# Eight 32 by 64 places of the array at once, and 32 by 32 turns, in the setup of an attention kernel

## The chip, the cores and the metric

The kernel runs on one core of a Trainium2 chip. The metric is the time of one execution on the device, in microseconds (us). The core has five engines that run their own instruction streams and meet in semaphores: TensorE (PE, with its weight loads shown apart as PEld), VectorE (DVE), ScalarE (ACT), GpSimd (POOL) and SyncE (SP), whose queue starts most of the DMAs.

## The reference

One transformer layer over x of shape (4, 1024, 128), all in float32: attention with 16 heads of 64 and a bias by distance, a layer norm, a gated feed-forward part with a token shift, and a second layer norm. Each part's result is added to its input ahead of its layer norm.

```python
q, k, v = jnp.einsum('bsx,xMnd->Mbnsd', x, qkv)
a = jnp.einsum('bnsd,bntd->bnst', q, k) * q.shape[-1] ** (-0.5)
cum = jnp.cumsum(rpe_bias[:, :s], axis=-1)
bias = jnp.where(rel >= 0, cum[:, jnp.clip(rel, 0)], PAD)
a = jax.nn.softmax(a + bias, axis=-1)
mix = jnp.einsum('bnst,bntd->bnsd', a, v)
return jnp.einsum('bnsd,ndx->bsx', mix, out_w)
...
x_prev = jnp.concatenate([jnp.zeros((B, 1, C), x.dtype), x[:, :-1, :]], axis=1)
xr = mu_r * x + (1.0 - mu_r) * x_prev
xk = mu_k * x + (1.0 - mu_k) * x_prev
r = jax.nn.sigmoid(jnp.einsum('btc,dc->btd', xr, W_r))
k = jnp.einsum('btc,dc->btd', xk, W_k)
k_act = jnp.square(jax.nn.relu(k))
out = r * jnp.einsum('btc,dc->btd', k_act, W_v)
```

## The kernel before

The work is cut into 32 pair steps: 4 batches by 8 pairs of heads. Each step has 16 slots, one for each head and each tile of 128 query rows. In a slot TensorE makes the scores of a row tile four slots ahead (L1098), VectorE adds the bias and takes the row minimum (L769), ScalarE takes the exponential (L567), TensorE transposes the result (L1115), VectorE and ScalarE empty the banks (L787, L585), and TensorE multiplies with v (L1139) and projects q, k and v of the next pair (L1073, L1078). The order is written out by hand in one function for each engine, and every engine's stream starts with its part of the setup. All 32 steps stand behind that setup: whatever makes it longer or shorter moves them as a block.

The setup is the stretch that the change touches. These are its parts, in the order in which TensorE runs them:

- L1001: two turns of the relative bias (16 rows). L738 on VectorE copies the result.
- L1008: eight transposes of 128 by 128 that turn the tiles of x, four for each half. They wait for the two DMAs of x. L745 on VectorE and L612 on ScalarE copy the halves to `x_cur`.
- L1013: two products with only 16 output rows, the running sum of the bias. L747 copies the result, SP writes it to DRAM (L343) and reads it back in shifted rows as the bias table (L339).
- L1054: the projections of the first pair ("twin"), four of them, then the first scores (L1098), then four more. They need `x_cur` and the weights that L741 on VectorE lays out.

VectorE's stream before the change is: two memsets of the bias row (L734, L735), the copy L738, the two copies of L741, L745, L747, and then the low parts of the first pair (L848, L852) between the first bias rows (L769).

A float32 product stands in the profile as two matmul records and two weight loads; a transpose of float32 data in L1008 is one record.

Of the kernel before, what the change touches and what calls it, by code (L numbers as in the profile page):

```python
# [10 lines left out]
HEADS, D, SPAN = 16, 64, 256  # L11
P = 128
PAIRS = HEADS // 2
PAIR_STEPS = BATCH * PAIRS
TILES = SEQ // P
GROUP = 4
NEAR = SPAN + P
FAR = SEQ - NEAR
BANK = 512
# [5 lines left out]

ROWS = [(h, i) for g in range(TILES // GROUP) for h in range(2) for i in range(GROUP * g, GROUP * g + GROUP)]
NROWS = len(ROWS)
# [13 lines left out]
def score_at(r):  # L41


    if r < NROWS // 2:
        return BANK * (r % 4)
    width = P * (ROWS[r][1] + 1)
    return SEQ * (r % 2) + ((SEQ - width) // 2 if width - BANK < SHORTEST else 0)


def score_end(r):  # L50
    return score_at(r) + P * (ROWS[r][1] + 1 if ROWS[r][1] >= GROUP else GROUP)

# [42 lines left out]
def build(nc, x, qkv, out_w, rpe, w_r, w_k, w_v, mu_r, mu_k, out):  # L95


    seq_d = nc.dram_tensor("bias_by_distance", (HEADS, 4 * P), F32, kind="Internal").ap()
    toeplitz = bass.AP(seq_d.tensor, 0, [[4 * P, HEADS], [1, P], [1, NEAR]])
    mix_d = nc.dram_tensor("mix_transposed", (PAIR_STEPS, P, SEQ), F32, kind="Internal").ap()  # L100
    inv_d = nc.dram_tensor("inverse_sums", (2, 2, 2 * GROUP, P), F32, kind="Internal").ap()
    xt_d = nc.dram_tensor("x_transposed", (BATCH, P, SEQ), F32, kind="Internal").ap()
# [7 lines left out]
    with ExitStack() as ctx:  # L110
        def sb(name, shape, dt=F32):
            return ctx.enter_context(nc.sbuf_tensor(name, shape, dt))

        def ps(name, shape):
            return ctx.enter_context(nc.psum_tensor(name, shape, F32))

        def sem(name):
            return ctx.enter_context(nc.semaphore(name))
# [6 lines left out]
        ident = sb("ident", [P, P])  # L125
# [15 lines left out]
        inv = sb("inv", [P, NROWS])  # L141
        inv_t = [sb(f"inv_t{g}", [2 * GROUP, P]) for g in range(2)]
        inv_all = [sb(f"inv_all{g}", [P, GROUP * P]) for g in range(2)]
        pt = [[sb(f"pt{h}{g}", [P, GROUP * (g + 1), GROUP * P]) for g in range(2)] for h in range(2)]
        mix_sb = [sb(f"mix_sb{g}", [P, GROUP * P]) for g in range(2)]
# [40 lines left out]
        ps_rows = ps("ps_rows", [P, 2 * SEQ])  # L186
# [8 lines left out]
        s_const = sem("const")  # L195
# [18 lines left out]
        s_w_twin = sem("twin_weights")  # L214
        s_twin = sem("twin_projected")
        s_twin_hi = sem("twin_hi_ready")
        s_twin_lo = sem("twin_lo_ready")
        s_stack = [sem(f"stacked{h}") for h in range(2)]
        s_table = [[sem(f"table{a}{h}") for h in range(2)] for a in range(2)]
# [108 lines left out]
        def _(sp):  # L328
# [7 lines left out]
            def load_table(n):  # L336

                for h in range(2):
                    sp.dma_start(table[n % 2][:, h, 0:NEAR], toeplitz[n % PAIRS * 2 + h, :, :])\  # L339
                        .then_inc(s_table[n % 2][h], 16)  # L340
# [133 lines left out]
        def _(pool):  # L474
# [11 lines left out]
            for a in range(2):  # L486
                pool.memset(table[a][:, :, NEAR:], 0.0).then_inc(s_zero, 1)
            pool.memset(x1_t[:, 0:1], 0.0).then_inc(s_zero, 1)
# [233 lines left out]
        def _(dve):  # L722
# [11 lines left out]
            nc.vector.memset(seq_sb[:, 0:P - 1], MASKED).then_inc(s_seq, 1)  # L734
            nc.vector.memset(seq_sb[:, P - 1 + SPAN:], 0.0).then_inc(s_seq, 1)  # L735

            dve.wait_ge(s_rpe_t, 1)
            nc.vector.tensor_copy(rpe_t, ps_t[0][:, 0:2 * HEADS].rearrange("p (a n) -> p a n", a=2)).then_inc(s_rpe_t, 1)  # L738
            dve.wait_ge(s_w[0], 16)
# [256 lines left out]
        def _(pe):  # L996
# [3 lines left out]
            for a in range(2):  # L1000
                ins = nc.tensor.transpose(ps_t[0][:, HEADS * a:HEADS * a + HEADS],  # L1001
                                          pt[0][0][0:HEADS, 0, P * a:P * a + P], ident[0:HEADS, 0:HEADS])
            ins.then_inc(s_rpe_t, 1)

            for first in (0, GROUP):
                pe.wait_ge(s_in_x[first // GROUP], 16)
# [5 lines left out]
            for a in range(2):  # L1012
                ins = nc.tensor.matmul(ps_t[1][0:HEADS, 0:SPAN], rpe_t[:, a, :], above[:, a, :],  # L1013
                                       start=(a == 0), stop=(a == 1))
# [88 lines left out]
            def transpose(n, r, tile_too):  # L1103
                pe.wait_ge(s_exp, NROWS * n + r + 1)
                for k in (k for k in range(NBANKS) if BANKS[k][0] == r):
                    _, b0, nb = BANKS[k]

                    if TBANK[k] == 2 and 2 not in TBANK[:k]:
                        pe.wait_ge(s_raw, 2 * n + 2)
                    else:  # L1110
                        engine, count = emptied(n, k)
                        pe.wait_ge(s_ev[engine], count)
                    for b in range(nb):
                        at = P * (b0 + b)
                        ins = nc.tensor.transpose(t_bank[TBANK[k]][:, P * b:P * b + P].bitcast(F32R),  # L1115
                                                  prob_r[:, r % PSLOTS, at:at + P], ident_r[:, :])
                    if k in INV_BANK:
                        g = INV_BANK.index(k)
                        pe.wait_ge(s_inv, 2 * n + g + 1)
                        ins = nc.tensor.transpose(t_bank[TBANK[k]][0:2 * GROUP, 3 * P:],  # L1120
                                                  inv[:, 2 * GROUP * g:2 * GROUP * (g + 1)], ident[:, :])
                    if k == X1_BANK and tile_too:
                        pe.wait_ge(s_chain, CH * (n - TILE_LAG + 1) + 4)
                        ins = nc.tensor.transpose(t_bank[TBANK[k]][:, P:2 * P], x1[:, :], ident[:, :])
                    ins.then_inc(s_tr, 1)
# [171 lines left out]
```

## Time and profile before

| | before |
|---|---|
| median of the runs | 1114.47 us (1114.06 to 1114.88, 2 runs) |
| the profiled execution | 1114.79 us |
| its span on the core | 1113.0 us |
| TensorE matmul busy | 1062.6 us, 95% of the span |
| TensorE weight loads | 751.8 us, 68% |
| ScalarE | 779.6 us, 70% |
| VectorE | 753.3 us, 68% |
| GpSimd | 97.3 us, 9% |

The span runs from the first instruction to the last; 1.8 us of the execution's time lie around it. Busy time of TensorE counts overlapping matmuls once. "Released by" in a row is what ended the idle time ahead of it. Times in rows are us from the span's start, and a row may hold several instructions of one line, merged: it then gives the start of the first and the time that all of them cover.

### The profile page before, as it was taken

What the parts mean: (1) busy time and instruction counts of PE and PEld (TensorE: products, weight loads), DVE (VectorE), ACT (ScalarE), POOL (GpSimd) and SP (SyncE); (2) the same over time, 40 slices, a digit from 0 to 9 for tenths busy, and PEclk for the clock granted to TensorE, in tenths of its full rate; (3) what the DMA queues carried; (4) which work ended last, traced back from release to release, by engine and by line L of the source; (5) the groups of instructions that cost most, each with busy time, mean ns of one, the idle gap of its engine ahead of it and who ended that gap; (6) DMA issues with size and microseconds to landing.
All of it is one profiled execution on the core that took longest, in us unless ns stands there. A gap on an engine that the chain in (4) does not pass through costs nothing.

```text
span 1113.0 us, 21807 instructions
## 1 busy us (share of the span) xinstructions
PE 1062.6 (95%) x6983; PEld 751.8 (68%) x6983; DVE 753.3 (68%) x1983; ACT 779.6 (70%) x2002; POOL 97.3 (9%) x103
## 2 busy tenths in 40 slices
PE   7899999999999999999999999999999999999995
PEld 4665666666666777676777676677676677666774
DVE  5665556666666777676777776767766667776667
ACT  4766677776767777777777776777676777777743
POOL 1000000000000111000011100011100011100100
PEclk9999999999999999999999999999999999999997
DMA  3765575675667677667676666776766676765810
GB/s 96 182 152 161 162 178 143 167 185 135 163 156 175 163 169 171 167 157 182 162 179 159 173 155 160 170 181 167 178 153 159 166 185 148 184 158 151 245 61 21
DMA packets 114319, 177.58 MB, mean 160 GB/s; under 512 B 13312, under 2 KB 72592, under 8 KB 114208
## 3 DMA queue, kind: packets, MB, share of 16 engines
q1 hardware_dynamic: 111648, 175.08, 63.2%
q10 hardware_dynamic: 2560, 1.12, 0.4%
q8 instruction: 58, 0.95, 0.4%
q14 instruction: 53, 0.43, 0.1%
HBM read 58.41 MB, written 20.22 MB: 71 GB/s over the span
## 4 chain that ended last, share of the span: by engine, by line
PE 61%; DMA 6%; ACT 5%; SPq 5%; issue 4%; DVE 3%; POOL 1%; DVEq 0%
PE ps_o L1139 19%; PE ps_rows L1098 15%; PE ps_t L1115 8%; PE ps_m L1073 7%; DMA stacks<-k_lo 6%; PE ps_m L1155 4%; SPq L323 4%; PE ps_m L1078 3%; ACT prob L567 3%; PE ps_o L1115 2%; ACT pt L585 2%; POOL mix_sb L496 1%; DVE pt L787 1%; PE ps_rows L1200 1%; SPq L388 1%
## 5 line engine op out<-in xcount | busy, mean ns | idle before, releaser
L769 DVE CUSTOM_DVE_ANT_0 prob<-ps_rows,table 128x128 f32<-128x128 f32 (+7 forms) x512 | 379.9, 750 | 96.6 <-PE ps_rows L1098 84.6
L567 ACT ACTIVATE prob<-prob,low 128x128 f32<-128x128 f32 (+7 forms) x512 | 394.4, 772 | 41.1 <-DVE low L769 37.0
L1098 PE MATMUL ps_rows<-stacks 128*128 128x512 f32 (+3 forms) x1536 | 393.4, 367 | 11.3 <-DMA stacks<-k_lo 9.3
L1115 PE MATMUL ps_t<-ident_r,prob_r 128*128 128x128 f32 x1984 | 282.9, 262 | 6.5 <-ACT pt L585 2.5
L1115 PEld LDWEIGHTS ps_t<-ident_r,prob_r 128*128 128x128 f32 x1984 | 212.2, 141 | 87.3 <-issue 71.4
L1139 PE MATMUL ps_o<-pt,v_pair 128*64 128x512 f32 (+3 forms) x1536 | 269.8, 493 | 0.0
L1098 PEld LDWEIGHTS ps_rows<-stacks 128*128 128x128 f32 x1536 | 244.5, 189 | 32.9 <-DMA stacks<-k_lo 13.9
L787 DVE COPY pt<-ps_t 128x512 f32<-128x512 f32 (+3 forms) x288 | 165.1, 583 | 147.1 <-PE ps_t L1115 146.9
L1139 PEld LDWEIGHTS ps_o<-pt,v_pair 128*64 128x64 f32 x1536 | 102.0, 137 | 177.1 <-issue 164.8
L585 ACT ACTIVATE pt<-ps_t 128x512 f32<-128x512 f32 (+3 forms) x384 | 175.1, 456 | 32.3 <-PE ps_t L1115 31.4
L496 POOL TENSOR_TENSOR mix_sb<-mix_sb,inv_all 128x512 f32<-128x512 f32 x64 | 82.2, 1284 | 922.0 <-ACT mix_sb L609 922.0
L1073 PE MATMUL ps_m<-x_cur,w_cur 128*128 128x512 f32 x248 | 129.4, 603 | 5.6 <-ACT x_t L539 2.6
L552 ACT ACTIVATE q_hi<-ps_m 128x512 fp32r<-128x512 f32 x62 | 36.7, 592 | 120.1 <-PE ps_m L1073 119.8
L567 ACT ACTIVATION_READ_ACCUMULATOR prob<-prob,low 128x1 f32 x512 | 98.3, 192 | 0.0
L755 DVE SCALAR_TENSOR_TENSOR q_lo<-ps_m,q_hi 128x512 fp32r<-128x512 f32 x62 | 42.8, 691 | 53.3 <-ACT q_hi L552 53.3
L1078 PEld LDWEIGHTS ps_m<-w_cur,x_cur 128*128 128x128 f32 x504 | 65.5, 191 | 3.2 <-issue 0.5
L1078 PE MATMUL ps_m<-w_cur,x_cur 128*128 128x128 f32 x504 | 66.3, 274 | 0.0
L583 ACT ACTIVATE inv_t<-ps_t 8x128 f32<-8x128 f32 x64 | 16.8, 262 | 63.2 <-PE ps_o L1139 59.5
L1073 PEld LDWEIGHTS ps_m<-x_cur,w_cur 128*128 128x128 f32 x248 | 42.2, 188 | 17.0 <-issue 7.2
L1115 PE MATMUL ps_o<-ident_r,prob_r 128*128 128x128 f32 x320 | 43.9, 252 | 5.4 <-DVE pt L787 5.3
L755 DVE SCALAR_TENSOR_TENSOR k_lo<-ps_m,k_hi 128x512 fp32r<-128x512 f32 x62 | 42.7, 689 | 7.1 <-ACT k_hi L552 4.7
L1155 PE MATMUL ps_m<-wo,mix_tile 128*128 128x128 f32 x384 | 47.0, 275 | 0.0
(131 smaller groups left out, 690.8 us busy)
## 6 DMA issues: line engine op xcount, KB each, us to landing
stacks<-k_hi SPq DMA_DIRECT2D x124, 256.0 KB, 4.5
stacks<-k_lo SPq DMA_DIRECT2D x124, 256.0 KB, 5.0
inv_all<-inverse_sums SPq DMA_DIRECT2D x128, 128.0 KB, 3.2
stacks<-q_hi SPq DMA_DIRECT2D x62, 256.0 KB, 3.7
stacks<-q_lo SPq DMA_DIRECT2D x62, 256.0 KB, 4.3
mix_transposed<-mix_sb SPq DMA_DIRECT2D x62, 256.0 KB, 3.7
table<-bias_by_distance SPq DMA_DIRECT2D x64, 192.0 KB, 3.8
mix_tile<-mix_transposed SPq DMA_DIRECT2D x24, 448.0 KB, 3.9
```

The costliest lines, as they stand in the source:

```text
L496: nc.gpsimd.tensor_tensor(mix_sb[g][:, :], mix_sb[g][:, :], inv_all[g][:, :], ALU.mult).then_inc(s_o, 1)
L567: nc.scalar.activation(row, row, ACT.Exp, bias=low[:, r:r + 1], scale=-1.0, accum_out=total[:, r:r + 1]).then_inc(s_exp, 1)
L585: nc.scalar.activation(pt[h][g][:, b0:b0 + nb, P * (i % GROUP):P * (i % GROUP) + P], t_bank[TBANK[k]][:, 0:nb * P].rearrange("p (b s) -> p ...
L755: nc.vector.scalar_tensor_tensor(out=lo[:, half], in0=proj_bank(m, c), scalar=scale, in1=hi[:, half].bitcast(F32), op0=ALU.mult, op1=ALU.s ...
L769: nc.vector.tensor_tensor_reduce(prob[:, r % PSLOTS, 0:width], ps_rows[:, score_at(r):score_at(r) + width], table[n % 2][:, h, 0:width][:, ...
L787: nc.vector.tensor_copy(pt[h][g][:, b0:b0 + nb, P * (i % GROUP):P * (i % GROUP) + P], t_bank[TBANK[k]][:, 0:nb * P].rearrange("p (b s) -> ...
L1073: ins = nc.tensor.matmul(proj_bank(m, c), w_cur[m % 2][:, which, :], x_cur[:, 512 * at:512 * at + 512], start=True, stop=True)
L1078: ins = nc.tensor.matmul(proj_bank(m, c)[:, P * t:P * t + P], x_cur[:, at:at + P], w_cur[m % 2][:, 2, :], start=True, stop=True)
L1098: ins = nc.tensor.matmul(ps_rows[:, at + c0:at + c1], q_st(h, n)[:, P * i:P * i + P], k_st(h, n, low_part)[:, c0:c1], start=(low_part == 0 ...
L1115: ins = nc.tensor.transpose(t_bank[TBANK[k]][:, P * b:P * b + P].bitcast(F32R), prob_r[:, r % PSLOTS, at:at + P], ident_r[:, :])
L1139: ins = nc.tensor.matmul(ps_o[D * h:D * h + D, c0:], v_pair[n % 2][:, j, D * h:D * h + D], pt[h][g][:, j, c0:], start=(j == 0), stop=(j == ...
L1155: ins = nc.tensor.matmul(ps_m[:, 0:C], mix_tile[:, p, :], wo[:, p, :], start=(p == 0), stop=(p == PAIRS - 1))
```

## The change

The change adds work and takes nothing away. On VectorE, behind the two first memsets, it adds four instructions: a turn of the identity in 32 by 32 blocks (128 by 128 elements), a memset of two rows of 512 float32 in each of 128 partitions, which releases TensorE by a new semaphore, and two more turns in 32 by 32 blocks (of 1024 and of 512 elements in each partition). On TensorE, behind L1001 and ahead of the transposes of x, it adds 256 float32 products. Each reads 32 rows of the identity as weights (64 columns) and 32 rows of the memset data, and writes 64 partitions of one of the four banks of `ps_rows`. One turn has eight products, four row groups by two column halves of the array; there are 16 turns with 128 columns, 8 with 256 and 8 with 64. Nobody reads their results: the banks are written again by the transposes of x, and the data tile `pt[0][1]` is first written by real work in the first pair step.

```diff
+QUARTER = 32
...
+        s_ramp = sem("ramp")
...
             nc.vector.memset(seq_sb[:, P - 1 + SPAN:], 0.0).then_inc(s_seq, 1)
 
+            probe = pt[0][1]
+            dve.wait_ge(s_const, 2)
+            nc.vector.transpose(probe[:, 3, 0:P], ident[:, :])
+            nc.vector.memset(probe[:, 0:2, :], 1.0).then_inc(s_ramp, 1)
+            dve.wait_ge(s_ramp, 1)
+            nc.vector.transpose(probe[:, 4:6, :].rearrange("p a n -> p (a n)"), probe[:, 0:2, :].rearrange("p a n -> p (a n)"))
+            nc.vector.transpose(probe[:, 6, :], probe[:, 0, :])
...
             ins.then_inc(s_rpe_t, 1)
 
+            pe.wait_ge(s_ramp, 1)
+            ramp = pt[0][1][:, 0, :]
+            for columns_moved, rounds in ((P, 16), (2 * P, 8), (D, 8)):
+                for turn in range(rounds):
+                    for quarter in range(P // QUARTER):
+                        rows = slice(QUARTER * quarter, QUARTER * quarter + QUARTER)
+                        for h in range(2):
+                            bank = ps_rows[D * h:D * h + D, BANK * quarter:BANK * quarter + columns_moved]
+                            nc.tensor.matmul(bank, ident[rows, D * (turn % 2):D * (turn % 2) + D],
+                                             ramp[rows, 0:columns_moved], start=(turn == 0), stop=(turn == rounds - 1))
```

TensorE's stream at its beginning, before the change (a row is a line, the tile written and those read, the output's shape, and how many stand there):

```order
L1001 MATMUL ps_t<-ident,pt 128x16 x2
L1008 MATMUL ps_rows<-ident,prob 128x128 x8
L1013 MATMUL ps_t<-pt 16x256 x2
L1054 MATMUL ps_m<-x_cur,pt 128x512
L1054 MATMUL ps_o<-x_cur,pt 128x512
L1054 MATMUL ps_t<-x_cur,pt 128x512 x2
L1098 MATMUL ps_rows<-stacks 128x256 x4
```

The same place after it (the lines are numbered anew: L1029 is L1008, L1034 is L1013 and L1075 is L1054 of before):

```order
L1011 MATMUL ps_t<-ident,pt 128x16 x2
L1023 MATMUL ps_rows<-pt,ident 64x128 x128
L1023 MATMUL ps_rows<-pt,ident 64x256 x64
L1023 MATMUL ps_rows<-pt,ident 64x64 x64
L1029 MATMUL ps_rows<-ident,prob 128x128 x8
L1034 MATMUL ps_t<-pt 16x256 x2
L1075 MATMUL ps_m<-x_cur,pt 128x512
```

All 256 products stand ahead of the first transpose of x, and nothing behind them is reordered.

VectorE's stream at its beginning, before the change:

```order
L734 MEMSET x_t 16x127
L735 MEMSET x_t 16x129
L738 COPY pt<-ps_t 128x32
L741 COPY pt<-w_cur 128x4x64 x2
L745 COPY x_cur<-ps_rows 128x512
L747 COPY x_t<-ps_t 16x256
```

The same place after it (L748, L751, L755 and L757 are L738, L741, L745 and L747 of before):

```order
L736 MEMSET x_t 16x127
L737 MEMSET x_t 16x129
L741 STREAM_TRANSPOSE pt<-ident 128x128
L742 MEMSET pt 128x1024
L744 STREAM_TRANSPOSE pt<-pt 128x1024
L745 STREAM_TRANSPOSE pt<-pt 128x512
L748 COPY pt<-ps_t 128x32
L751 COPY pt<-w_cur 128x4x64 x2
L755 COPY x_cur<-ps_rows 128x512
L757 COPY x_t<-ps_t 16x256
```

Four instructions come ahead of the copies of the setup. The streams of ScalarE, GpSimd and SP are as before.

## Rows read from the trace of the kernel before

**Rows 1.** The page: span, busy time by engine, granted TensorE clock in 40 slices.

```profile
span 1113.0 us, 21807 instructions
PE 1062.6 (95%) x6983; PEld 751.8 (68%) x6983; DVE 753.3 (68%) x1983; ACT 779.6 (70%) x2002; POOL 97.3 (9%) x103
PEclk9999999999999999999999999999999999999997
```

**Rows 2.** Timeline of PE, setup: start, covered us, engine, line, tiles, shape, count [idle before].

```profile
2.74 0.36 PE L1001 MATMUL ps_t<-ident,pt 16*128 16x16 f32 x2 [2.74 <-DMA pt<-in_L_attn_rpe_bias]
5.17 2.25 PE L1008 MATMUL ps_rows<-ident,prob 128*128 128x128 f32 x8 [2.06 <-DMA prob<-in_L_attn_x]
7.34 1.89 PE L1013 MATMUL ps_t<-pt 128*16 128x256 f32 x4
8.60 0.63 PE L1013 MATMUL ps_t<-pt 128*16 128x256 f32 x1
9.16 1.84 PE L1054 MATMUL ps_m<-x_cur,pt 128*128 128x512 f32 x2
10.84 1.02 PE L1054 MATMUL ps_o<-x_cur,pt 128*128 128x512 f32 x2
11.70 1.88 PE L1054 MATMUL ps_t<-x_cur,pt 128*128 128x512 f32 x4
13.32 1.55 PE L1098 MATMUL ps_rows<-stacks 128*128 128x256 f32 x8
```

**Rows 3.** Windows: every engine's busy us, granted clock (third from the end), DMA share, GB/s.

```profile
5.00:10.00 5.00, 4.82 (x13) 2.37 (x14) 1.79 (x4) 0.60 (x1) 0.35 (x4) 1.00 0.71 186
44.50:47.90 3.40, 3.40 (x25) 3.30 (x24) 2.20 (x9) 2.01 (x7) 0.00 (x0) 0.54 0.97 208
```

**Rows 4.** Timeline of PE in the first product with v, and what follows it.

```profile
39.36 2.38 PE L1139 MATMUL ps_o<-pt,v_pair 128*64 128x512 f32 x16
41.67 0.54 PE L1115 MATMUL ps_t<-ident_r,prob_r 128*128 128x128 f32 x4
```

**Rows 5.** Groups of instructions by shape in the same stretch, busy us, mean ns.

```profile
L1139 PE MATMUL ps_o<-pt,v_pair 128*64 128x512 f32 x4 | 1.1, 618 | 0.0
L1139 PE MATMUL ps_o<-pt,v_pair 128*64 128x128 f32 x4 | 0.4, 273 | 0.0
```

**Rows 6.** The page's DMA queues, then the DMA view of 34 to 36 us.

```profile
q8 instruction: 58, 0.95, 0.4%
q8 instruction: 1, 0.02, 3.2%
```

**Rows 7.** Timeline of DVE and POOL in the setup.

```profile
1.95 0.17 DVE L735 MEMSET x_t<- 16x129 f32 x1
1.81 0.52 POOL L482 MEMSET pt<- 128x512 f32 x1
2.97 2.27 POOL L487 MEMSET table<- 128x1280 f32 x2
3.72 1.96 DVE L741 COPY pt<-w_cur 128x256 f32<-128x256 f32 x2 [0.39 <-DMA w_cur<-in_L_attn_qkv]
5.41 0.27 DVE L741 COPY pt<-w_cur 128x256 f32<-128x256 f32 x1
6.32 0.69 DVE L745 COPY x_cur<-ps_rows 128x512 f32<-128x512 f32 x1 [0.63 <-PE ps_rows L1008]
```

**Rows 8.** Timeline, the bias table's way and the first rows that use it.

```profile
9.27 0.41 DVE L747 COPY x_t<-ps_t 16x256 f32<-16x256 f32 x1 [2.26 <-PE ps_t L1013]
9.71 0.33 SPq L343 DMA_DIRECT2D bias_by_distance<-x_t  x1
11.30 1.78 SPq L339 DMA_DIRECT2D table<-bias_by_distance  x4
14.85 0.28 DVE L769 CUSTOM_DVE_ANT_0 prob<-ps_rows,table 128x128 f32<-128x128 f32 x1
16.26 0.39 ACT L567 ACTIVATE prob<-prob,low 128x128 f32<-128x128 f32 x1
```

**Rows 9.** The table tile's view: time from a DMA's issue to its landing.

```profile
DMA to landing us min/median/max: 3.0/3.4/3.8
```

## The prediction

> **What bounds the kernel now.** The page first: TensorE's matmuls cover 1062.6 of 1113.0 us, and the clock row is 9 in every slice but the last [rows 1]. The kernel is bound by TensorE from the setup to the end, and the change adds to TensorE's stream ahead of everything. So the question is only how long the added block holds the setup up, and what the setup gives back. I read TensorE's timeline of the setup next [rows 2]: L1001 is over at 3.10, TensorE sits idle for 2.06 us until x has landed at 5.17, and from there to the first scores at 13.32 it has work almost without a gap. The only free cover for the new block is that idle stretch.
>
> The same rows give the clock. A record of L1013 has 256 columns; four start between 7.34 and 8.60, 0.42 us apart, or 1.64 ns a column. Records of L1054 have 512 columns; two start between 10.84 and 11.70, 0.43 us apart, or 0.84 ns a column, while the two before took from 9.16 to 10.84, 0.84 us each. The setup thus runs at the 1.2 GHz level until past 10 us and at 2.4 GHz after. The windows print a granted clock of 1.00 for 5 to 10 us [rows 3]; I go by the pace. Where the view does show the low level (0.54 in 44.5 to 47.9, behind a stall), it lasts a few us.
>
> **How long the new block streams.** It has 128 products of 128 columns, 64 of 256 and 64 of 64, each two records. Their columns sum to 2 x (16,384 + 16,384 + 4,096) = 73,728 record columns. One at a time at 0.833 ns that is 61.4 us; eight at once, 7.7 us. What does the trace say of records beside each other? L1139 writes the two column halves of 64: 16 records, four each of 512, 384, 256 and 128 columns [rows 4, 5], 5,120 columns in all, 4.27 us one after the other. They took from 39.36 to 41.67, 2.31 us. So two column halves run at once, in float32, and their two passes too. Row groups of 32 the trace never uses. The bounds are therefore two at once (30.7 us) and eight at once (7.7 us). I take eight: the row groups read their own partitions and write their own banks, as the column halves write their own partitions, and I see no shared part that L1139 shows to be full.
>
> The page "TensorE: Matmul & The Clock Gate" of the Trainium skill (Part 3, on packing small matmuls) says that tiles of separate row and column groups run together, 10.6 times as fast with 16 of them; no row here has row groups. The page (Part 1) also puts a floor of about 25 ns between the starts of matmuls. By that floor the 512 records would need 12.8 us where my sum has 7.7, and the whole would be some 5 us longer, an estimate from that page.
>
> **What comes on top.** (a) The clock. The block starts at the low level. In before that level held from the work at 5.17 to past 10; I take about 4.4 us of it here, which costs half, 2.2 us (bounds 0 and 7.7, all of it at the low level). (b) Loading code. TensorE's code comes in 58 packets of 0.95 MB, 16 KB each, for 13,966 records: some 240 to 256 instructions a packet. The one between 34 and 36 us used 3.2% of 16 engines in 2 us, 1.0 us of one [rows 6]. The block is 1,024 instructions, four packets, and at eight at once uses one up in 1.9 us. With a way of 1.6 us from issue (the distance of L343 to L339, [rows 8]) a packet takes 2.6 us, so two of the four may be late by 0.7 us. I take 1.0 us (bounds 0 and 4 x 2.6 = 10.4, all in turn). (c) The start. VectorE is free at 2.12. The 128 by 128 turn costs about what L735 costs for 129 elements, 0.17, at most 0.3. The memset of 1,024: POOL's of 512 took 0.52 and VectorE's copy L745 of 512 took 0.69 [rows 7], so 1.04 to 1.4 us. TensorE starts at about 3.5. The upper end is a block by POOL: L741's first copy ran from 3.72 to about 5.4 while POOL wrote the table (2.97 to 5.24), its second took 0.27 [rows 7]. Were the memset held like that, the start would come at 5.3 to 6.4, 2.4 us later on average.
>
> The page "SBUF — State Buffer" of the Trainium skill (Who interferes with whom) says that VectorE and GpSimd share a port pair which copies in a two-port mode need and a memset does not; L735 beside POOL's L482, 0.17 us, agrees. Without that page L735 alone speaks for 3.5.
>
> The block ends at 3.5 + 7.7 + 2.2 + 1.0 = 14.4.
>
> **What the setup gives back.** Behind the block x is there and the clock is high. The eight transposes, records of 128 columns, need 8 x 0.107 = 0.86 us, L1013 4 x 0.213 = 0.85, the eight records of L1054 ahead of the scores 8 x 0.43 = 3.44: 5.2 us with the start of a record, where before 5.17 to 13.32 took 8.15. The scores start at end + 5.2, so the shift is end - 8.1: 14.4 - 8.1 = **+6.3 us**.
>
> Two things could keep that gain back. VectorE's turns of 1024 and 512 elements cost 1.1 + 0.6 us at a memset's pace, at most 2.8 at twice the copy's; with L738 and L741 behind them VectorE is ready by 6 to 9 us, under the block's cover until 14.4. If the block ended by 8, that cover would be gone. The second is the bias table: L747, L343, L339 and 3.0 to 3.8 us to landing [rows 8, 9] are DMA latencies that no clock shortens. Last L1013 at end + 1.5, copy done 0.6 later, and 1.6 + 3.4 on: the table lands at end + 7.3, the first bias row was due at 14.85 - 8.1 = end + 6.75. It is 0.5 us late, and hidden: in before ScalarE took up its result only at 16.26, over 1 us after it stood [rows 8].
>
> All 32 pair steps move as a block. 1114.79 + 6.3 = 1121.1 for the profiled execution, which is 0.3 above the median: **1120.8 us**.
>
> **Rivals.** A difference under about 2% is what a measurement of this kernel can't tell from none; that is 22.3 us, a block of 26.9 us or more.
>
> *Row groups take turns (slower).* Only the two column halves overlap, as in L1139, the sole pattern the trace shows. The block streams 30.7 us plus 2 us of low clock and ends at 36.4: +28, 1142.8. A pace by records gives the same: L1139's shortest records, of 128 columns, come two in 107 ns by their columns, 54 ns a record, and 512 at 54 ns are 27.6 us, ending at 33.3, +25, 1139.7. For it: no row shows three at once. Against: the 54 ns are what the columns themselves need. It decides where fewer than about 2.5 of eight places work at once.
>
> *Four at once.* 15.4 + 2.2 ends at 21.1: +13, 1127.5.
>
> *The clock stays low.* If small places don't lift it, the block takes 15.4 us and the setup stays slow: end 18.9, and 18.9 - 5.17 = +13.7, 1128.2. For it: no such work stands ahead of a rise in the trace. Against: the rise in before came behind a stretch with L1013 in it, work of 16 output columns.
>
> *Nearly free.* All at the high level, no code wait: end 11.2, +3.1, 1117.6. A gain over before isn't in reach: even the whole 3 us given back and the 2.06 idle don't cover 7.7.
>
> **Chances.** Eight at once, with its free end, 0.62 (own range 1117 to 1125); four at once or a floor between, 0.13; clock low, 0.05; turns or pace by records, 0.17; else, below 1117 or faster by a shifted stall, 0.03. The range 1117 to 1130 leaves out the last two, 0.20, and holds a blocked start. Faster by over 2%: 0.01. Within 2%: 0.82. Slower by over 2%: 0.17.
>
> **What would show it.** In the timeline of after: the block's first record at about 3.5; its 512 records over 10 to 11 us, with starts a few ns apart in groups of eight; L1029 at about 14.4 with no wait for x; L1034 at 0.21 us a record; the first scores at about 19.6; the bias table's row 0.5 us behind; the later steps as before, shifted. A block of over 20 us shows the row groups wrong; gaps between turns with code packets in them, the code term too small; a start behind 5.2, the port. The prediction would also be wrong if a stall such as that at 44 us moved in or out of a low-clock stretch, worth up to 1.7 us each.

## The result, and the profile after

The changed kernel took 1128.2 us in its two first executions (1125.6 and 1130.8), a ratio to before of 1.0114 (1.0074 to 1.0154). With five more rounds it had 1122.7 us beside 1113.9 us for before, a ratio of 1.0089 (1.0061 to 1.0117). So it is some 10 us slower, about 1%, where 6.3 us were predicted. Both medians lie in the range; the likeliest value, 1120.8, was below them by 7.4 and 1.9 us.

The page of the profiled execution (1125.6 us), against [rows 1] and the first of [rows 6]: 1,028 more instructions, 512 more matmul records and four more packets of TensorE's code. Busy time of TensorE grew by 9.4 us.

```profile
span 1123.9 us, 22835 instructions
PE 1072.0 (95%) x7495; PEld 762.6 (68%) x7495; DVE 753.9 (67%) x1987; ACT 780.7 (69%) x2002; POOL 97.4 (9%) x103
q8 instruction: 62, 1.02, 0.4%
```

TensorE's timeline of the setup in the same execution, the answer to [rows 2]. L1023 is the added block; at the end of a row stands the idle time ahead of it and what ended it.

```profile
3.42 6.09 PE L1023 MATMUL ps_rows<-pt,ident 32*64 32x128 f32 x221 [0.46 <-DVE pt L742]
10.99 3.35 PE L1023 MATMUL ps_rows<-pt,ident 32*64 32x128 f32 x128 [1.48 <-issue]
14.99 2.42 PE L1023 MATMUL ps_rows<-pt,ident 32*64 32x256 f32 x128 [0.66 <-issue]
19.00 0.66 PE L1023 MATMUL ps_rows<-pt,ident 32*64 32x64 f32 x35 [1.58 <-issue]
19.59 1.97 PE L1029 MATMUL ps_rows<-ident,prob 128*128 128x128 f32 x8
21.48 1.70 PE L1034 MATMUL ps_t<-pt 128*16 128x256 f32 x4
23.11 1.12 PE L1075 MATMUL ps_m<-x_cur,pt 128*128 128x512 f32 x2
26.56 1.54 PE L1119 MATMUL ps_rows<-stacks 128*128 128x256 f32 x8
```

The block starts at 3.42, as forecast, and ends at 19.6, not 14.4. It is cut three times, behind 221, 349 and 477 records, and each time the profile finds nothing that TensorE waits for ("issue"). Between two cuts stand 128 records and their 128 weight loads, 256 instructions. The first scores start at 26.56, 13.2 us behind before's 13.32.

How dense the block is in its first piece, and what the clock did behind the third cut, is in the windows (columns as in [rows 3]):

```profile
3.40:9.40 6.00, 5.98 (x221) 5.85 (x221) 2.31 (x5) 0.00 (x0) 1.94 (x5) 1.00 0.91 240
19.60:23.00 3.40, 3.40 (x13) 1.98 (x12) 0.69 (x1) 0.60 (x1) 0.00 (x0) 0.52 0.03 5
```

221 records in 6.0 us are 27 ns each. At the low level (the pace of L1013 in before, 1.67 ns a column) one record of 128 columns takes 213 ns, so eight were in the array at once. Four at once at the high level would look the same here; the second piece rules that out. Its 93 records of 256 columns also come 27 ns apart, and one of them needs 213 ns even at the high level, the fastest pace in any row. The trace's list of clock changes has the rise at 9.21, as the first piece ends, and the fall at 19.45. The second row is the low clock again, 0.52 over the 3.4 us in which the real setup runs its transposes.

VectorE's timeline shows the added instructions (the answer to [rows 7]):

```profile
2.05 0.24 DVE L741 STREAM_TRANSPOSE pt<-ident 128x128 f32<-128x128 f32 x1
2.46 0.91 DVE L742 MEMSET pt<- 128x1024 f32 x1 [0.17 <-issue]
3.40 1.25 DVE L744 STREAM_TRANSPOSE pt<-pt 128x1024 f32<-128x1024 f32 x1
4.57 0.67 DVE L745 STREAM_TRANSPOSE pt<-pt 128x512 f32<-128x512 f32 x1
5.24 0.47 DVE L751 COPY pt<-w_cur 128x256 f32<-128x256 f32 x2
20.73 0.69 DVE L755 COPY x_cur<-ps_rows 128x512 f32<-128x512 f32 x1 [15.02 <-PE ps_rows L1029]
```

The memset, from 2.46 to 3.37, ran beside GpSimd's work (its memset of the table starts at 2.97) and took 0.91 us, so it was not held, and VectorE then waited 15 us for TensorE. The two copies of L751 took 0.47 us in place of 1.96; they now start at 5.24, when GpSimd's memsets of the table are over.

### The profile page after: what moved, and what is told of

Read it like the earlier page. It is cut to its first block, busy times and chain, and to the rows that moved or that the text cites. A ratio compares the mean times of both kernels' runs of the same rounds, so it can differ in the third digit from the quotient of the medians.

```text
span 1123.9 us, 22835 instructions
## 1 busy us (share of the span) xinstructions
PE 1072.0 (95%) x7495; PEld 762.6 (68%) x7495; DVE 753.9 (67%) x1987; ACT 780.7 (69%) x2002; POOL 97.4 (9%) x103
## 4 chain that ended last, share of the span: by engine, by line
PE 58%; DMA 7%; SPq 7%; ACT 5%; issue 4%; DVE 3%; POOL 2%; DVEq 0%
PE ps_o L1160 19%; PE ps_rows L1119 14%; PE ps_t L1136 8%; DMA stacks<-k_lo 7%; PE ps_m L1094 7%; SPq L325 6%; PE ps_m L1176 4%; PE ps_m L1099 3%; ACT prob L569 3%; PE ps_o L1136 2%; POOL mix_sb L498 2%; ACT pt L587 1%; DVE pt L797 1%; PE ps_rows L1221 1%; SPq L390 1%
```

## The experiments

The theory after the first profile of the changed kernel: the eight places do work at once; what the sum lacked is the loading of TensorE's code, which comes one packet of 256 instructions at a time, and a clock that falls behind such a wait. Rivals: the cuts were a single accident; the row groups or the columns cost it; VectorE's added work does; the difference comes from later steps.

All kernels below are the changed kernel or the kernel before, as they are or with one edit.

### The changed kernel once more

> The changed kernel once more. Theory (code and clock): every execution has the three waits of 0.7 to 1.6 us inside the block, behind records 221, 349 and 477, because TensorE's code comes in packets of 256 instructions about 3.9 us apart; the block ends near 19.6 and the first scores start near 26.5, 13 us later than before; the median is 9 to 14 us above before. Rival (the packets came late once, behind the loads of x): the block ends at 15 to 17 and the median is at most 8 us above before.

The ratio was 1.0089 (1.0061 to 1.0117), +9.9 us by the ratio. Its timeline of TensorE:

```profile
3.42 5.08 PE L1023 MATMUL ps_rows<-pt,ident 32*64 32x128 f32 x221 [0.41 <-DVE pt L742]
10.49 3.35 PE L1023 MATMUL ps_rows<-pt,ident 32*64 32x128 f32 x128 [1.98 <-issue]
14.21 2.42 PE L1023 MATMUL ps_rows<-pt,ident 32*64 32x256 f32 x128 [0.38 <-issue]
17.67 0.62 PE L1023 MATMUL ps_rows<-pt,ident 32*64 32x64 f32 x35 [1.03 <-issue]
18.22 1.10 PE L1029 MATMUL ps_rows<-ident,prob 128*128 128x128 f32 x8
23.66 1.55 PE L1119 MATMUL ps_rows<-stacks 128*128 128x256 f32 x8
```

The three cuts stand behind the same records, 3.4 us in all against 3.7, so they are no accident. Two things differ. The clock rose earlier (the first 221 records took 5.08 us and not 6.09), and it did not fall behind the third cut: the transposes took 1.10 us and not 1.97, and from the block's end to the scores it was 5.4 us against 7.0. The same kernel thus puts the first scores at 26.56 or at 23.66. By an estimate from these rows, 2.6 us of the difference are the clock (1.1 by the earlier rise, 1.5 behind the block) and 0.3 us are shorter waits. The scores at 26.5 that were expected came 2.9 us sooner: the three waits repeat, the clock does not.

### The same columns in a quarter of the instructions

```diff
-            for columns_moved, rounds in ((P, 16), (2 * P, 8), (D, 8)):
+            for columns_moved, rounds in ((4 * P, 9),):
```

> The block as 9 turns of 512 columns: the same 36,864 product columns in 144 records and 288 instructions in place of 512 and 1,024. Theory (code): no packet wait in the block, which streams from 3.4 to about 14.1 (6 us of it at the low clock, 1.7 us a turn, then 0.85 us a turn); no low-clock stretch behind it; scores at 19.3, a shift of 6 us in place of 13. Rival (the columns cost it): the block ends near 19 as in the changed kernel, a shift of 12 to 13 us.

TensorE's timeline:

```profile
3.42 9.58 PE L1023 MATMUL ps_rows<-pt,ident 32*64 32x512 f32 x144 [0.49 <-DVE pt L742]
12.94 1.09 PE L1029 MATMUL ps_rows<-ident,prob 128*128 128x128 f32 x8
18.37 1.54 PE L1119 MATMUL ps_rows<-stacks 128*128 128x256 f32 x8
```

No cut, the block ends at 12.94, and the scores start 5.05 us behind before; the ratio was 1.0043 (1.0013 to 1.0073), +4.8 us by the ratio. The end comes 1.2 us ahead of the 14.1 expected: the clock rose at 6.73, 3.3 us behind the start, and not after 6 us. The block's columns are the same as in the changed kernel. So the columns cost about 5 us, and the other 5 to 8 us of the shift come with the 1,024 instructions: the waits, a floor on small records, and in the first profile a later rise and a fall of the clock.

### The same instructions with 11% of the columns

```diff
-            for columns_moved, rounds in ((P, 16), (2 * P, 8), (D, 8)):
+            for columns_moved, rounds in ((16, 32),):
```

> The block as 32 turns of 16 columns: the same 512 records and 1,024 instructions, 11% of the columns. Theory (code): the packets set it; three waits, the last packet about 8 us behind the first, the block ends at 15.5 to 18 and the scores start at 22 to 26. Rival (the columns cost it): 4,096 columns stream in 1.7 us at the low clock, the block ends by 6, the scores start by 14.5.

TensorE's timeline:

```profile
3.42 3.23 PE L1023 MATMUL ps_rows<-pt,ident 32*64 32x16 f32 x221 [0.52 <-DVE pt L742]
9.06 1.97 PE L1023 MATMUL ps_rows<-pt,ident 32*64 32x16 f32 x128 [2.41 <-issue]
12.51 1.97 PE L1023 MATMUL ps_rows<-pt,ident 32*64 32x16 f32 x128 [1.49 <-issue]
15.97 0.82 PE L1023 MATMUL ps_rows<-pt,ident 32*64 32x16 f32 x35 [1.49 <-issue]
16.72 1.97 PE L1029 MATMUL ps_rows<-ident,prob 128*128 128x128 f32 x8
23.70 1.55 PE L1119 MATMUL ps_rows<-stacks 128*128 128x256 f32 x8
```

The cuts stand behind the same 221, 349 and 477 records, and the pieces start 3.5 us apart (9.06, 12.51, 15.97) though each has only 1.7 us of work. The block ends at 16.7 in place of 18.2 to 19.6: nine tenths of the columns are worth 1.5 to 3 us. The DMA view has one code packet in 10 to 12 us and one in 13 to 15 us, that is one for each piece:

```profile
q8 instruction: 1, 0.02, 3.1%
q8 instruction: 1, 0.02, 3.3%
```

3.1% of 16 engines in 2 us is 1.0 us for the transfer. The other 2.5 us of the 3.5 are not transfer. The trace has each packet's start, and it shows what the 3.5 us consist of (us from the span's start; the run without the turns stands further down; its piece at 13.42 waited only 0.11 us):

| run | the packets start | the pieces' first records |
|---|---|---|
| changed kernel | 8.51, 12.36, 16.37 | 10.99, 14.99, 19.00 |
| once more | 8.14, 11.59, 15.34 | 10.49, 14.21, 17.67 |
| 16 columns | 6.49, 10.18, 13.63 | 9.06, 12.51, 15.97 |
| without the turns | 7.40, 10.99, 14.51 | 9.96, 13.42, 16.87 |

A piece's first record runs 2.3 to 2.6 us behind the start of its packet, and the next packet starts 1.0 to 1.4 us behind that record. The two add up to the 3.5 to 4.0 us between pieces. Why the first packet starts at 6.5 in one run and at 8.5 in another is open; the DMA engines were nearly full with x and the weights at that time (0.91 in the row of 3.4 to 9.4 above), and no run was made without that load.

### Only the 128-column turns

```diff
-            for columns_moved, rounds in ((P, 16), (2 * P, 8), (D, 8)):
+            for columns_moved, rounds in ((P, 16),):
```

> Only the 16 turns of 128 columns: 256 records, 512 instructions. Theory (code and clock): one wait for a packet behind record 221 as in the whole block, the other 35 records by 12, scores at about 17.2, a shift of 4 us. Rival (the products themselves are slow, in proportion to their columns): the block has 44% of the columns, and the shift would be 44% of 13, 5.9 us, with no gap in it.

TensorE's timeline:

```profile
3.42 5.90 PE L1023 MATMUL ps_rows<-pt,ident 32*64 32x128 f32 x221 [0.44 <-DVE pt L742]
11.29 0.87 PE L1023 MATMUL ps_rows<-pt,ident 32*64 32x128 f32 x35 [1.96 <-issue]
12.09 1.97 PE L1029 MATMUL ps_rows<-ident,prob 128*128 128x128 f32 x8
19.14 1.54 PE L1119 MATMUL ps_rows<-stacks 128*128 128x256 f32 x8
```

The windows of the same execution, behind the cut:

```profile
12.00:15.40 3.40, 3.40 (x15) 2.00 (x12) 0.69 (x1) 0.60 (x1) 0.00 (x0) 0.51 0.02 5
```

The cut is there, 1.96 us long behind record 221, and the block ends at 12.1 as the theory has it. The shift of the scores is 5.8 us, though, not 4: that number fits the rival, its "no gap" does not. That row shows why: the clock was low again (0.51) right behind the cut, over the transposes. 3.4 us at that level cost 1.7 us, which takes the 17.2 expected to 18.9, near the 19.14 found. The time was 1122.0 us, ratio 1.0069 (1.0043 to 1.0095).

### All four quarters on one row group

```diff
-                        rows = slice(QUARTER * quarter, QUARTER * quarter + QUARTER)
+                        rows = slice(0, QUARTER)
```

> As the changed kernel, but all four quarters read rows 0 to 31, so that only the two column halves are different places; banks, columns and instructions are unchanged. Theory (row groups work at once in the changed kernel): now they take turns, 30.7 us of streaming and 2 to 3 of low clock, the block ends at 36 to 38, the scores start near 43. Rival (the place in the array did not matter, the code did): the block ends near 19.6 again.

The block's groups by shape (busy us, mean ns of one), without its last 128 records:

```profile
L1023 PE MATMUL ps_rows<-pt,ident 32*64 32x128 f32 x256 | 27.6, 416 | 0.5 <-DVE pt L742 0.5
L1023 PE MATMUL ps_rows<-pt,ident 32*64 32x256 f32 x128 | 27.5, 629 | 0.0
```

TensorE's timeline of the same execution:

```profile
65.06 1.97 PE L1029 MATMUL ps_rows<-ident,prob 128*128 128x128 f32 x8
72.48 1.55 PE L1119 MATMUL ps_rows<-stacks 128*128 128x256 f32 x8
```

The block now ends at 65.1, and this single execution took 1170.6 us. The 256 records of 128 columns took 27.6 us: half of 32,768 record columns at 1.67 ns is 27.3, so two ran at once, and at the low level. In the changed kernel the same instructions, on four row groups and at the same low level, are four times as dense: 27 ns a record where 27.6 us over 256 are 108 ns. That is the direct proof that row groups work side by side. No cut stands in this block: 128 records take about 7 us and more here, and the code keeps up. My number for this run, 36 to 38, was wrong by the clock: it did not rise at all in 61 us in which TensorE was never idle, and I had counted it low for 6 us.

### VectorE's part alone, and TensorE's part alone

The first keeps VectorE's four instructions and leaves the products and their wait out; the second keeps the products and the memset and leaves the three turns out.

```diff
-            pe.wait_ge(s_ramp, 1)
-            ramp = pt[0][1][:, 0, :]
-            for columns_moved, rounds in ((P, 16), (2 * P, 8), (D, 8)):
...
```

> VectorE's four added instructions alone, no products on TensorE. Theory: VectorE is through with them and L738 and L741 by 5.7, ahead of the first half of x at 6.3, so the scores start within 0.3 us of 13.3 and the time is that of before. Rival (they hold VectorE, or GpSimd through the shared port): scores later than 14, GpSimd's memsets of the table longer than 1.2 us each.

```diff
-            nc.vector.transpose(probe[:, 3, 0:P], ident[:, :])
             nc.vector.memset(probe[:, 0:2, :], 1.0).then_inc(s_ramp, 1)
-            dve.wait_ge(s_ramp, 1)
-            nc.vector.transpose(probe[:, 4:6, :].rearrange("p a n -> p (a n)"), probe[:, 0:2, :].rearrange("p a n -> p (a n)"))
-            nc.vector.transpose(probe[:, 6, :], probe[:, 0, :])
```

> The changed kernel without the three turns on VectorE; its memset and the whole block on TensorE stay. Theory (the block sets it alone): three waits for code, the block ends at 18 to 20, scores at 23 to 27, the ratio that of the changed kernel, 1.006 to 1.012. Rival (the turns hold something up): the ratio falls to under 1.005.

VectorE's part alone: ratio 0.9978 (0.9959 to 0.9997), scores at 12.44. TensorE's part alone: ratio 1.0063 (1.0036 to 1.0090), scores at 22.85. GpSimd's two memsets of the table took 2.27 us in the first, as in before. So the turns by themselves cost nothing that shows, and the block without them costs most of it or all: the intervals of 1.0063 and of the changed kernel's 1.0089 overlap, so a small part of the turns in the whole is neither shown nor excluded. That the scores of the first start 0.9 us ahead of before is more than I expected; in that execution x had landed at 4.73 and not at 5.17, and the clock rose at 9.31 and not at 10.64. I did not find out whether VectorE's turns have a part in that. TensorE's timeline in the second:

```profile
3.25 5.65 PE L1018 MATMUL ps_rows<-pt,ident 32*64 32x128 f32 x221 [0.23 <-DVE pt L741]
9.96 5.88 PE L1018 MATMUL ps_rows<-pt,ident 32*64 32x128 f32 x256 [1.07 <-issue]
16.87 0.62 PE L1018 MATMUL ps_rows<-pt,ident 32*64 32x64 f32 x35 [1.03 <-issue]
```

Only two cuts show as idle time, where three were expected. The trace has the third: record 350 starts at 13.42, 0.48 us behind the one before it and 0.11 us behind the last end, too little for a row of its own. The block ends at 17.4 and the scores start at 22.85, both a little ahead of what was expected (18 to 20 and 23 to 27): the first packet came sooner, at 7.40, and the clock did not fall behind a cut.

### A block that fits under the wait for x

Four turns of 128 columns, 64 records, in place of the whole block (run twice); and eight turns fed from the identity, put ahead of L1001 in the kernel before, with nothing on VectorE.

```diff
-            for columns_moved, rounds in ((P, 16), (2 * P, 8), (D, 8)):
+            for columns_moved, rounds in ((P, 4),):
```

> Only 4 turns of 128 columns: 64 records, 128 instructions, no packet wait. Theory: the block runs 3.4 to 5.2, under the wait for x, at the low clock; scores at 11.7 to 13.5 against 13.3 before, the gain being what an earlier rise of the clock gives back (0 to 1.7 us); a median within 2 us of before. Rival (VectorE's added work or the switch of array shape costs by itself): scores at 14.5 or later.

> The block of 4 turns once more, with more rounds. Theory (an early rise of the clock gives back up to 1.7 us of setup): ratio 0.998 to 0.9995, scores at 11.6 to 12.5. Rival (the 0.9975 of the first time was chance): ratio within 0.9995 to 1.001.

```diff
             pe.wait_ge(s_const, 2)
+            for turn in range(8):
+                for quarter in range(4):
+                    rows = slice(32 * quarter, 32 * quarter + 32)
+                    for h in range(2):
+                        bank = ps_rows[D * h:D * h + D, BANK * quarter:BANK * quarter + P]
+                        nc.tensor.matmul(bank, ident[rows, D * (turn % 2):D * (turn % 2) + D],
+                                         ident[rows, :], start=(turn == 0), stop=(turn == 7))
             pe.wait_ge(s_identr, 1)
```

> The kernel before with 8 turns of 128 columns put ahead of L1001, fed from the identity alone, so that they can start at 1.6 and fill the whole wait for x; nothing added on VectorE. Theory: 128 records at the low clock take 3.4 us, end at 5.0 to 5.3, the clock has risen by 7.5, and scores start at 10.5 to 11.7, about 2 us ahead of before: ratio 0.9975 to 0.999. Rival (an early code packet or the later L1001 eats it): scores at 12.5 or later.

The timeline of the first run of four turns:

```profile
3.42 2.01 PE L1023 MATMUL ps_rows<-pt,ident 32*64 32x128 f32 x64 [0.53 <-DVE pt L742]
5.37 1.90 PE L1029 MATMUL ps_rows<-ident,prob 128*128 128x128 f32 x8
7.20 1.04 PE L1034 MATMUL ps_t<-pt 128*16 128x256 f32 x4
11.61 1.54 PE L1119 MATMUL ps_rows<-stacks 128*128 128x256 f32 x8
```

The transposes of x start at 5.37, no later than x lands in before, and L1034 already runs at the high level, 1.04 us against 1.89. The scores start at 11.61, in the second run at 11.97, and in the kernel with eight early turns at 11.56, where before had 13.32 and, in two more profiles, 13.74 and 12.95 (next section). The ratios are 0.9975 (0.9952 to 0.9997), 0.9980 (0.9956 to 1.0003) and 0.9988 (0.9967 to 1.0010). The setup is shorter by 1.3 to 1.8 us against the first profile of before (1.0 to 2.2 against all three), which is 0.15% of the time; the whole time can't show it with certainty, as the next section has it.

### What a ratio is worth here

The kernel before was profiled twice more, one of them in five rounds against itself.

> The kernel before once more, to see how far one program's executions drift apart behind the setup. Theory: the first scores start within 0.3 us of 13.3, and later pair steps differ by up to 3 us from the execution profiled before, as stalls on the stacked operands' DMAs come and go with low-clock stretches behind them. Rival (the drift seen between before and after comes from the change): all steps agree within 0.5 us.

> The kernel before against itself. It shows what a ratio of this kernel is worth: theory, that single times scatter by 5 us either way for reasons behind the setup, gives a ratio within 0.9975 to 1.0025 and an interval that holds 1 or misses it narrowly; the rival, that the intervals of the other runs can be taken as they stand, gives 0.9995 to 1.0005.

Against itself it had 0.9995 (0.9972 to 1.0018), with single times from 1108.6 to 1120.5 us. The scores of the two profiles started at 13.74 and 12.95, beside 13.32, a little outside the 0.3 us expected. Behind the scores (span less their start) its three executions took 1095.9, 1099.1 and 1099.7 us, and the changed kernel's two 1097.3 and 1094.6. So one and the same program drifts by almost 4 us behind the scores, and the changed kernel lies within 1.3 us of that band. The biggest waits there are those on the stacked operands' DMAs. In the waits view of the first profile (us in total, times, longest), for before:

```profile
PE ps_rows L1098 <- DMA stacks<-k_lo: 9.3, 15, 1.5
```

and for the changed kernel:

```profile
PE ps_rows L1119 <- DMA stacks<-k_lo: 9.8, 18, 1.7
```

The six later times of the changed kernel lay between 1120.0 and 1127.6. So of the first two, 1125.6 is high but within them and 1130.8 lies above them all, and 1114.5 for before was a good middle. The shift of the scores, 10.3 to 13.2 us in the two profiles, has less chance in it.

## Why the prediction was right, and where its sum was off

**The time alone would not have settled it.** The first median of 1128.2 is the very number of the rival "the clock stays low" (1128.2) and near that of "four at once" (1127.5); my 1120.8 was further off. The range held it because its upper end, 1130, was set wide for a blocked start and for those rivals, not for the waits that came. What was right is the mechanism of the block, and that is read from the timeline.

**Eight at once: right.** The block's pace of 27 ns a record at the low level, the same pace for 256 columns at the high level, and the one-row-group kernel, settle it; the rival of turns is out, and so is four at once, whose 15.4 us is more than the 9.58 us of the block with 512 columns. With 144 long records the block ended at 12.94, near my bare 3.5 + 7.7 + 2.2 = 13.4. "The clock stays low" is out for the changed kernel (it rose at 9.21 and at 6.96), but its condition did come true in two variants: with 16 columns and with one row group the clock stayed low to the block's end.

**The start at 3.5: right** (3.42). VectorE's memset took 0.91 us and was not held by GpSimd. The turns took 0.24, 1.25 and 0.67 us, under cover. (The 2.8 us given as their most is not what its words work out to: 1,536 elements at twice L745's time for each are 4.1 us. Nothing hung on it.)

**The code term: mis-sized, 1.0 against 3.4 to 3.7 us of idle time, 4.2 to 4.5 with the drain of the records ahead of each cut.** The step that failed is "a packet takes 2.6 us, so two of the four may be late by 0.7 us". The 2.6 us themselves, put together from a transfer and the way of another DMA, were right: 2.3 to 2.6 us from a packet's start to its first record. What I put at nothing is the time ahead of that start. The next packet starts only 1.0 to 1.4 us after the piece ahead of it has begun to run, so the pieces start 3.5 to 4.0 us apart, with 1.7 us of work in a piece (16 columns) or with 3 us of it (the first full piece of the changed kernel). Each piece that holds less work than that leaves TensorE idle: three pieces were late, not two, by 0.4 to 2.4 us each (0.1 us in one case), and not by 0.7. The q8 row [rows 6] gave the transfer only.

**The low clock: 4.4 us against 5.8 and 3.5** in the two profiled executions. In the first all 221 records of the first piece came at the low pace, 5.8 us; in the second they came in 4.8 us, 27 ns apart for 3.5 us and some 14 ns apart for the rest. The 4.4 had no row behind it: the reading of [rows 2], low from 5.17 until past 10, gives 5 us or more (the rise in before stands at 10.64). It lies between the two by luck.

**A floor on records: missing.** Records of 16 columns come 13.4 ns apart at the low clock (3.23 us less 0.26 of one record's own length, over 221). The 128 records of 64 columns, at the high clock, would need 6.7 ns by their columns and come 10 to 12 ns apart, with a pause of 0.2 us where the width changes; so this costs about 0.8 us. The 13.4 ns are a quarter of the 54 ns of my rival. The page "TensorE: Matmul & The Clock Gate" of the Trainium skill (Part 1) gives a floor of about 25 ns; the records here come at half of that and less, so the measurement decides against it for products in separate places. The 5 us that I estimated from that page would have brought my number close to the measured one, but by a cause that is not there.

**What the setup gives back: right in one execution, lost in the other.** From block's end to scores I had 5.2 us. It was 5.4 in the second profile and with long records (12.94 to 18.37), but 7.0 in the first, where the clock fell behind the third cut. I had named the code wait and the clock each by itself and not asked whether the clock might fall behind a wait. It did so in two executions, this one and the one with only the 128-column turns. In the second profile and without VectorE's turns there were such waits and no fall; with 16 columns the clock had not risen; and no kernel without waits had a fall in the setup. So the waits make it possible; that they alone cause it is not shown.

Together, for the first profile: 0.7 us from the clock's rise, 3.5 from code, 0.8 from the floor, 1.8 from the clock behind the cut, 6.8 us in all, which takes the forecast shift of 6.3 to 13.1, with 13.2 found. In the second profile it is 10.3: the clock's rise gave back 0.4, the three waits were shorter (3.2 us over the forecast), and there was no fall behind them.

**The bias table: right.** Its first row came at 28.29 in the first profile, 1.73 us behind the scores where before had 1.53, and the next VectorE work still waited for ScalarE. The forecast's sum had a slip: 1.5 + 0.6 + 1.6 + 3.4 is 7.1 us behind the block's end, not 7.3, so the row was due 0.35 us late, not 0.5; it was 0.2 late.

**No pair step but by the block: as far as the runs can tell.** Behind the scores changed and unchanged kernels lie in one band. The forecast class, within 2%, held. No cost of the turns or of the port shows in any run.

## What to carry to other kernels

A burst of small instructions on TensorE can be bound by the loading of its code and not by the array, as this one was: read how many packets the engine's code has in the whole run, work out instructions per packet, and compare the burst's time for that many instructions with about 4 us. The same columns in 512-wide products cost half as much here. A wait inside such a burst may also cost the clock of the real work behind it (in two of the four executions here in which it had risen), so a filler should end within the wait that covers it; the ones that did moved the first scores ahead by 1.3 to 1.8 us. And where several rivals give nearly the same time, decide beforehand which row of the timeline tells them apart.

## What the runs showed of the hardware

- Float32 products of 32 rows by 64 columns in all eight places run at once: 27 ns a record of 128 columns at the low level, against 213 ns for one alone. A common row group leaves two at once.
- Records of 16 columns with their weight loads come 13.4 ns apart at the low clock; records of 64 columns 10 to 12 ns apart at the high one, where their columns alone would need 6.7.
- TensorE's code comes 256 instructions at a time. Once the first stock is used, pieces start no less than 3.5 to 4 us apart: 1.0 to 1.4 us until the next packet starts, 2.3 to 2.6 us from there to its first record, of which 0.9 to 1.2 us is transfer. Pieces with about 7 us of work or more (one row group) show no wait.
- The clock did not rise in 61 us of unbroken work on one row group of 32. It was also still low for the setup behind the 16-column block: its L1029 took 1.97 us for the eight transposes. With all four row groups at 128 columns it had risen after 3.5 to 5.8 us.
- The windows print a granted clock of 1.00 for stretches ahead of the first change that they know of. In the one-row-group kernel they say 1.00 for 4 to 60 us, where the pace is that of the low level, and the first change in the trace's list is a rise at 69.34. The pace is the thing to go by:

```profile
4.00:60.00 56.00, 56.00 (x418) 43.58 (x416) 1.71 (x5) 0.00 (x0) 1.35 (x5) 1.00 0.08 23
```
